# A graph network's edge stage: the order of a chunk's steps within and across slots, on one core

## The chip, the core and the metric

The kernel runs on one core of a Trainium2 chip. The metric is device time in microseconds, the median of several executions; smaller is better. The engines of the core are TensorE (PE in the profile, its weight loads PEld), VectorE (DVE), ScalarE (ACT), GpSimd (POOL) and SyncE (SP), each with its own instruction stream; they meet only at semaphores.

## What is computed

```python
# x (12500, 64), src, dst (400000,), dst sorted, edge_attr_16 (400000, 16)
x = layernorm(x + L0(x, src, dst))      # three graph convolutions with degree norms and ELU
x = layernorm(x + L1(x, src, dst, edge_attr_16))

# L1, of which the edge stage is the first three lines
ea = edge_attr @ W_edge.T + b_edge
msg = relu(x[src] + ea)                 # one message of 64 numbers for each of 400000 edges
agg = segment_sum(msg, dst, 12500)
h = (x + agg) @ W1.T + b1               # then batch statistics, relu, @ W2.T + b2
```

The destinations are skewed: node numbers are 12500 times the square of a uniform number, so the first nodes have many more edges than the last.

## The kernel before, in words

The first convolutions (L0) are done with dense matrices of edge counts, in the first 4650 us or so. While they run, the edges of the first 5 windows of 512 nodes are written out again, sorted by the block of 128 source nodes. The edge stage then takes the edges in two ways, interleaved.

A **unit** is 5 tiles of 128 edges, in the order given, for the later windows. GpSimd gathers the source rows from DRAM with 5 indirect DMAs (`gather_units`, L1086), into one of 6 row buffers. TensorE makes the edge term from the attributes (`unit_edges`, L2271), VectorE adds the gathered rows to it (`add_rows`, L1652) and builds 5 one-hots of the destination (`unit_hots`, L1660), ScalarE and VectorE split the rectified message in two halves of 16 bits (`unit_high`, L1934; `unit_low`, L1665), and TensorE adds them into the window's sums (`unit_sums`, L2285). There are 345 units. GpSimd may gather unit n once `add_rows` of unit n - 6 is done.

A **chunk** is 8 or 6 tiles of the sorted edges, 294 in all, 147 of each size. Its source rows come from a table in SBUF through a one-hot, not by a DMA. The steps, by helper:

- `prepare` (VectorE, L1634, L1637, L1638): the source's digit and the destination from the records.
- `spread_digits` (TensorE, L2304), in two halves of up to four tiles, both into one PSUM bank: each tile's digits spread over 128 partitions. `src_hot` turns them into one-hots: VectorE the first half (L1645), ScalarE the second in two steps (L1924, L1928). The second half of the spread waits for VectorE's `src_hot`, the next chunk's first half for ScalarE's.
- `chunk_flat` (ScalarE, L1908), `turn_attr` (TensorE, L2315), `chunk_attr` (ScalarE, L1917): the attributes, turned.
- `chunk_terms` (TensorE, L2324 and 12 or 16 times L2331): edge terms plus source rows. `chunk_high` (ScalarE, L1899) and `chunk_low` (VectorE, L1680): the two message halves.
- `chunk_hots` (VectorE, L1673, one of 512 columns for each tile): node one-hots. `chunk_sums` (TensorE, L2344, one for each tile): the sums.

The order of all this is written out by hand: each engine loops over slots n, one slot for each unit, and in 294 of them also stands work on chunks. `STEP_OF` spreads the chunks evenly, so about every seventh slot has none; `CHUNK_IN` gives the chunk of a slot. Most buffers of a chunk exist twice, and every helper begins with its waits. `ENDS_IN` says in which slot a window's sums are closed, multiplied by W1 and put into the batch statistics. SP loads attributes (L892) and records (L900), three ahead.

## Time and profile before

| | |
|---|---|
| median of 3 runs | 7608.19 us (7603.3 to 7616.36) |
| the profiled execution, first to last instruction (span) | 7586.7 us |
| mean granted TensorE clock over the span | 0.862 |
| PE / DVE / ACT / POOL busy | 73% / 56% / 30% / 50% of the span |
| DMA, mean | 109 GB/s |

The profiled execution's own time is given by its span alone; the median of the runs is 21.5 us above it. The page has the busy shares by slices of the span; a table of stretches gives busy times between two moments; groups put instructions of one line together; a timeline lists single instructions, and behind each what ended the idle time before it ("remote": something that the profile does not tell). TensorE's instructions overlap, and their ends are worked out by a model.

### The profile page before, as it was taken

Reading aid. Unit: us, or ns where it says so; the run is one execution under the profiler, and the core shown is the slowest. Engines: PE = TensorE matmul, PEld = TensorE weight load, DVE = VectorE, ACT = ScalarE, POOL = GpSimd, SP = SyncE. Lnnn points to the kernel's source line nnn. Section 1 sums busy time; section 2 is a strip of 40 time slices with the busy share of each in tenths; the row PEclk is TensorE's granted clock in tenths of the full one; section 3 lists DMA queues with packets and bytes.
Section 4 is the critical chain, followed back from the end, with each engine's and each line's share of the span. In section 5 each row is a group of like instructions: output and inputs, shape, how many; then the busy total and the mean of one; then the engine's idle time right before and its main releaser. Section 6 shows DMA issues by size and latency. Waiting matters only on the chain.

```text
span 7586.7 us, 112214 instructions
## 1 busy us (share of the span) xinstructions
PE 5556.9 (73%) x39907; PEld 3224.8 (43%) x39908; DVE 4274.3 (56%) x14548; ACT 2271.1 (30%) x4057; POOL 3774.9 (50%) x3824
## 2 busy tenths in 40 slices
PE   6599799997777777778777774666766666665666
PEld 5366566665433333333433332333433333333334
DVE  5488888899533333333444112666666665555556
ACT  2487688873100000000001111333333322222223
POOL 4323233354354544545554556565655666665663
PEclk9799899999888988888888886888888888878887
DMA  2333333331555655556556661111111111111111
GB/s 99 140 130 119 120 142 137 118 118 64 177 173 188 197 177 180 186 186 195 184 185 193 218 207 41 32 34 33 33 33 33 34 33 32 33 33 32 32 32 34
DMA packets 438341, 828.25 MB, mean 109 GB/s; under 512 B 161611, under 2 KB 266983, under 8 KB 430951
## 3 DMA queue, kind: packets, MB, share of 16 engines
q1 hardware_dynamic: 305430, 713.88, 27.9%
q0 software_dynamic: 117952, 81.54, 5.1%
q10 hardware_dynamic: 14400, 25.61, 1.2%
q8 instruction: 323, 5.29, 0.3%
q14 instruction: 236, 1.93, 0.1%
HBM read 621.34 MB, written 199.35 MB: 108 GB/s over the span
## 4 chain that ended last, share of the span: by engine, by line
PE 24%; another core or an unknown queue 14%; issue 13%; DVE 11%; PEld 2%; ACT 1%; PEldq 0%; DVEq 0%; ACTq 0%
PE banks L2182 10%; PE banks L2344 4%; DVE tmp L1673 4%; PE banks L2271 2%; PE banks L2304 2%; PEld banks L2182 2%; DVE onehot L1660 2%; DVE rows_f L1652 2%; PE banks L2324 2%; PE banks L2331 1%; PE banks L2164 1%; DVE rows_f L1680 1%; DVE rows_f L1665 1%; PE banks L2157 1%
## 5 line engine op out<-in xcount | busy, mean ns | idle before, releaser
L1086 POOL DMA_INDIRECT rows_f<-table,src_key x1725 | 1708.4, 990 | 1103.4 <-DVE rows_f L1652 604.3
L1051 POOL DMA_INDIRECT sorted_recs<-onehot,rows x1280 | 1235.5, 965 | 1260.6 <-DMA onehot<-edge_recs_dram 718.7
L2182 PE MATMUL banks<-wide,rows_f 128*128 128x512 fp8e4 (+1 forms) x4900 | 1268.1, 400 | 355.4 <-issue 352.3
L1867 ACT ACTIVATE wide<-banks 128x784 fp8e4<-128x784 f32 x1563 | 1205.6, 825 | 484.6 <-PE banks L2104 340.6
L1006 POOL DMA_INDIRECT onehot<-edge_runs_dram,rows_f x472 | 596.2, 1263 | 1149.1 <-DVE onehot L1196 935.9
L2104 PE MATMUL banks<-rows_f 128*128 128x196 f16 (+2 forms) x7525 | 1004.1, 258 | 223.6 <-ACT wide L1867 138.7
L2104 PEld LDWEIGHTS banks<-rows_f 128*128 128x128 f16 x7525 | 708.5, 152 | 612.1 <-ACT wide L1867 401.9
L2271 PE MATMUL banks<-w_edge_blk,rows 80*128 80x320 f32 x690 | 337.4, 578 | 762.9 <-DVE rows_f L1652 521.6
L1444 DVE SCALAR_TENSOR_TENSOR onehot<-banks,onehot 128x98 f16<-128x98 f32 (+2 forms) x1113 | 295.6, 266 | 989.9 <-PE banks L2164 504.1
L1342 DVE TENSOR_TENSOR rows_f<-hid 128x1024 f16<-128x1024 f16 (+1 forms) x1016 | 679.4, 669 | 300.8 <-PE banks L2104 169.5
L1645 DVE TENSOR_SCALAR rows_f<-banks,iota_p 128x512 f16<-128x512 f32 x294 | 220.7, 751 | 1067.0 <-remote 638.8
L2182 PEld LDWEIGHTS banks<-wide,rows_f 128*128 128x128 f16 x4900 | 454.9, 103 | 817.2 <-issue 510.3
L2069 PE MATMUL banks<-wide,onehot 128*128 128x392 fp8e4 x3125 | 791.5, 334 | 9.2 <-issue 8.9
L2182 PE MATMUL banks<-wide,hid 128*128 128x512 fp8e4 (+1 forms) x2450 | 650.1, 401 | 126.3 <-issue 125.2
L1347 DVE TENSOR_TENSOR rows_f<-rows_f,tmp 128x1568 f16<-128x1568 f16 (+1 forms) x874 | 714.4, 817 | 0.0
L2344 PE MATMUL banks<-tmp,rows_f 128*128 128x512 f16 x2058 | 676.6, 485 | 0.0
L1673 DVE TENSOR_SCALAR tmp<-iota_win,rows 128x512 f16<-128x512 f16 x2058 | 638.0, 379 | 0.0
L1899 ACT ACTIVATE rows_f<-banks 128x512 f16<-128x512 f32 (+1 forms) x294 | 160.0, 544 | 1146.8 <-remote 671.6
L2271 PEld LDWEIGHTS banks<-w_edge_blk,rows 80*128 80x128 f32 x690 | 126.0, 228 | 825.3 <-issue 824.7
L2157 PE MATMUL banks<-onehot 128*128 128x98 f16 (+2 forms) x1113 | 244.1, 219 | 160.2 <-DVE onehot L1444 101.1
L2344 PEld LDWEIGHTS banks<-tmp,rows_f 128*128 128x128 f16 x2058 | 233.5, 120 | 295.3 <-issue 198.3
L1660 DVE TENSOR_SCALAR onehot<-iota_win,dst_key 128x224 f16<-128x224 f16 x1725 | 353.6, 287 | 0.0
(345 smaller groups left out, 7312.1 us busy)
## 6 DMA issues: line engine op xcount, KB each, us to landing
wide<-counts SPq DMA_DIRECT2D x504, 896.0 KB
counts<-wide SPq DMA_DIRECT2D x50, 3136.0 KB
rows_f<-table,src_key POOLq DMA_INDIRECT x1725
sorted_recs<-onehot,rows POOLq DMA_INDIRECT x1280
sorted_recs<-rows SPq DMA_DIRECT2D x28, 640.0 KB
rows<-attr_dram SPq DMA_DIRECT2D x345, 40.0 KB
onehot<-edge_recs_dram SPq DMA_DIRECT2D x143, 90.0 KB
agg_a<-attr_dram ACTq DMA_DIRECT2D x50, 250.0 KB
```

Of the source, the lines that this page charges most:

```text
L1006: G.indirect_dma_start(out=stage[:, c % STAGES, j, :], out_offset=None, in_=edge_runs[:, :], in_offset=bass.IndirectOffsetOnAxis(ap=run_id ...
L1051: G.indirect_dma_start(out=sorted_recs[:, :], out_offset=bass.IndirectOffsetOnAxis(ap=keys_of(t, t + 1).bitcast(I32), axis=0), in_=taken[g ...
L1086: G.indirect_dma_start(out=g_rows[:, n % ROW_RING, k, :], out_offset=None, in_=table32[:, :], in_offset=bass.IndirectOffsetOnAxis(ap=src_k ...
L1342: V.tensor_tensor(lo_ring[:, s, :, 0:size], iota_lots[:, :, 0:size], lo_cols[:, n:lot.end].rearrange("p (o n) -> p o n", o=1).to_broadcast ...
L1347: V.tensor_tensor(key_ring[:, s, 0:size * cells].rearrange("p (n j e) -> p n j e", n=size, e=2), iota_key[:, 0:cells].rearrange("p (o j e) ...
L1673: last = V.tensor_scalar(c_hot[:, s, k, :], iota_win[:, :], c_dst[:, s, k:k + 1], None, ALU.is_equal)
L1867: A.activation(win_counts[o.half % 2][:, :, d0:d0 + o.quads * QUAD].rearrange("p b (q c) -> p b q c", c=QUAD), counted, ACT.Copy, scale=UN ...
L2069: M(out_ps.rearrange("p (b d) -> p b d", d=QUAD), ident16[:, :], win_counts[o.half % 2][:, :, d0:d0 + QUAD], start=False, stop=False)
L2104: last = M(octet_ps[n % 2][:, q, at:at + item.width * BLOCKS], lo, key, start=fresh[q], stop=True, skip_group_check=True)
L2182: last = M(acc_d[m % 2].rearrange("p (h d) -> p h d", h=2)[:, 0:h, :], layer_rows[n][:, block, :], pieces[:, PLACE[k], 0:h, c * HALF:(c + ...
L2271: M(g_ps, g_attr[:, n % ATTR_RING, :], w_edge_blk[0:UNIT * EDIM, 0:UNIT, :].rearrange("p k f -> p (k f)"), start=True, stop=True).then_inc ...
L2344: last = M(c_acc, c_two[:, s, k, :], c_hot[:, s, k, :], start=False, stop=False)
```

## The change

Three hand-written loops are reordered, on VectorE, ScalarE and TensorE; no instruction's size changes. In the slot of chunk j:

- TensorE spreads both halves of chunk j's digits (before: chunk j + 1's), with `unit_sums`, `unit_edges` and `turn_attr` between them, then makes the sums of chunk j - 2 (before: of j, after its terms), and last the terms of chunk j (before: first).
- VectorE begins with `add_rows` of the unit, then `src_hot(j)`, `chunk_low(j - 1)`, the unit's work, `chunk_hots(j - 1)` and `prepare(j + 1)`. Before, a slot began with `prepare(j + 1)`, `chunk_hots(j)` and `src_hot(j + 1)`, and `chunk_low(j)` followed `add_rows`.
- ScalarE makes `chunk_high(j - 1)`, and `src_hot(j)` in place of `src_hot(j + 1)`.
- There are two slots more, for the sums of the last two chunks.

```diff
--- before.py
+++ after.py
@@ -302,8 +302,11 @@
 
 CHUNKS_S = plan_chunks()
 
-STEP_OF = [n * GATHERS // len(CHUNKS_S) for n in range(len(CHUNKS_S))]
-CHUNK_IN = {step: j for j, step in enumerate(STEP_OF)}
+CHUNKS_N = len(CHUNKS_S)
+SUMS_LATER = 2
+STEP_OF = [n * GATHERS // CHUNKS_N for n in range(CHUNKS_N + SUMS_LATER)]
+SLOT_IN = {step: j for j, step in enumerate(STEP_OF)}
+STEPS = GATHERS + 1 + SUMS_LATER
 UNIT_NODES = 224
 
 
@@ -340,9 +343,9 @@
 UNIT_WINDOWS = [sorted({b // WIN, (b + UNIT_NODES - 1) // WIN}) for b in UNIT_BASE]
 BEGINS = {w: min(n for n in range(GATHERS) if w in UNIT_WINDOWS[n]) for w in range(SORTED, WINDOWS)}
 ENDS = {w: max(n for n in range(GATHERS) if w in UNIT_WINDOWS[n]) for w in range(SORTED, WINDOWS)}
-WINDOW_ENDS = sorted([(n + 1, 0, w) for w, n in ENDS.items()] + [(STEP_OF[j], 1, c.w) for j, c in enumerate(CHUNKS_S) if c.ends])
+WINDOW_ENDS = sorted([(n + 1, 0, w) for w, n in ENDS.items()] + [(STEP_OF[j + SUMS_LATER], 1, c.w) for j, c in enumerate(CHUNKS_S) if c.ends])
 END_OF = {w: q for q, (n, kind, w) in enumerate(WINDOW_ENDS)}
-ENDS_IN = {step: [q for q, e in enumerate(WINDOW_ENDS) if e[0] == step] for step in range(-1, GATHERS + 2)}
+ENDS_IN = {step: [q for q, e in enumerate(WINDOW_ENDS) if e[0] == step] for step in range(-2, STEPS)}
 
 LAST = 20
 ROW_RING, REC_RING, ATTR_RING, HOT_RING = 6, 4, 4, 4
@@ -907,8 +910,8 @@
                 for n in range(GATHERS):
                     if n + ATTR_RING - 1 < GATHERS:
                         load_attr(n + ATTR_RING - 1)
-                    if n in CHUNK_IN and CHUNK_IN[n] + REC_RING - 1 < len(CHUNKS_S):
-                        load_recs(CHUNK_IN[n] + REC_RING - 1)
+                    if n in SLOT_IN and SLOT_IN[n] + REC_RING - 1 < CHUNKS_N:
+                        load_recs(SLOT_IN[n] + REC_RING - 1)
 
             def unsorted_edges():
                 steps = sp.value_load(bounds[0:1, WINDOWS - 1, 1:2], min_val=1, max_val=WINDOWS * GRANULES)
@@ -1693,25 +1696,25 @@
                 gathered = dst_key[:, FIRST_UNIT * UNIT:].rearrange("p (g t) -> p g t", t=GRAN)
                 link(V.tensor_tensor(gathered, gathered, g_base.rearrange("p (g o) -> p g o", o=1).to_broadcast([P, len(BASES), GRAN]), ALU.subtract))
                 prepare(0)
-                src_hot(0)
                 dve.wait_ge(s_dtable, 16 * WINDOWS)
-                for n in range(GATHERS):
-                    j = CHUNK_IN.get(n)
-                    following = j is not None and j + 1 < len(CHUNKS_S)
-                    if following:
+                for n in range(STEPS):
+                    j = SLOT_IN.get(n)
+                    if n < GATHERS:
+                        add_rows(n)
+                    if j is not None and j < CHUNKS_N:
+                        src_hot(j)
+                    if j is not None and 1 <= j <= CHUNKS_N:
+                        chunk_low(j - 1)
+                    if n < GATHERS:
+                        unit_hots(n)
+                        unit_low(n)
+                    if j is not None and 1 <= j <= CHUNKS_N:
+                        chunk_hots(j - 1)
+                    if j is not None and j + 1 < CHUNKS_N:
                         prepare(j + 1)
-                    if j is not None:
-                        chunk_hots(j)
-                        if following:
-                            src_hot(j + 1)
-                    add_rows(n)
-                    if j is not None:
-                        chunk_low(j)
-                    unit_hots(n)
-                    unit_low(n)
-                    for q in ENDS_IN[n - 2] if n >= 1 else ():
-                        hidden_stats(q)
-                for n in range(GATHERS - 2, GATHERS + 2):
+                    for q in ENDS_IN[n - 2]:
+                        last = hidden_stats(q)
+                for n in range(STEPS - 2, STEPS):
                     for q in ENDS_IN[n]:
                         last = hidden_stats(q)
                 last.then_inc(s_tail, 1)
@@ -1948,19 +1951,17 @@
                 chunk_flat(0)
                 chunk_flat(1)
                 chunk_attr(0)
-                src_hot(0)
-                for n in range(GATHERS + 2):
-                    j = CHUNK_IN.get(n)
-                    following = j is not None and j + 1 < len(CHUNKS_S)
-                    if j is not None:
-                        chunk_high(j)
-                    if following:
-                        chunk_attr(j + 1)
+                for n in range(STEPS):
+                    j = SLOT_IN.get(n)
+                    if j is not None and 1 <= j <= CHUNKS_N:
+                        chunk_high(j - 1)
                     if n < GATHERS:
                         unit_high(n)
-                    if following:
-                        src_hot(j + 1)
-                    if j is not None and j + 2 < len(CHUNKS_S):
+                    if j is not None and j + 1 < CHUNKS_N:
+                        chunk_attr(j + 1)
+                    if j is not None and j < CHUNKS_N:
+                        src_hot(j)
+                    if j is not None and j + 2 < CHUNKS_N:
                         chunk_flat(j + 2)
                     for q in ENDS_IN[n - 1]:
                         window_hidden(q)
@@ -2361,28 +2362,27 @@
                 pe.wait_ge(s_dout, len(DENSE))
                 pe.wait_ge(s_x1two, X1TWO0 + 1)
                 unit_edges(0)
-                spread_digits(0, 0)
                 turn_attr(0)
-                spread_digits(0, 1)
-                for n in range(GATHERS + 2):
-                    j = CHUNK_IN.get(n)
-                    following = j is not None and j + 1 < len(CHUNKS_S)
-                    if j is not None:
-                        chunk_terms(j)
-                    if following:
-                        spread_digits(j + 1, 0)
-                        turn_attr(j + 1)
-                        turned[0] = j + 2
+                for n in range(STEPS):
+                    j = SLOT_IN.get(n)
+                    here = j is not None and j < CHUNKS_N
+                    if here:
+                        spread_digits(j, 0)
                     if 1 <= n <= GATHERS:
                         unit_sums(n - 1)
                     if n + 1 < GATHERS:
                         unit_edges(n + 1)
-                    if following:
-                        spread_digits(j + 1, 1)
+                    if here and j + 1 < CHUNKS_N:
+                        turn_attr(j + 1)
+                        turned[0] = j + 2
+                    if here:
+                        spread_digits(j, 1)
                     for q in ENDS_IN[n - 1]:
                         window_nodes(q)
-                    if j is not None:
-                        chunk_sums(j)
+                    if j is not None and j >= SUMS_LATER:
+                        chunk_sums(j - SUMS_LATER)
+                    if here:
+                        chunk_terms(j)
 
             pe.wait_ge(s_flag, 1)
             flagged = nc.tensor.value_load(flag[0:1, 0:1], min_val=0, max_val=1)
```

VectorE, a slot with a chunk of 8 tiles in the middle of the edge stage, before. `banks` is PSUM, `iota_win` and `iota_p` are counting numbers, `rows` holds digits and destinations. The row of L1645 is `src_hot`, the next one `add_rows`:

```order
7475 L1673 TENSOR_SCALAR tmp<-iota_win,rows 128x512 x8
7476 L1645 TENSOR_SCALAR rows_f<-banks,iota_p 128x512
7477 L1652 TENSOR_TENSOR rows_f<-banks,rows_f 128x320
7478 L1680 SCALAR_TENSOR_TENSOR rows_f<-banks,rows_f 128x8x64
7479 L1660 TENSOR_SCALAR onehot<-iota_win,dst_key 128x224 x5
7480 L1665 SCALAR_TENSOR_TENSOR rows_f<-rows_f 128x5x64
7481 L1634 TENSOR_SCALAR rows<-rows_f 128x8
7482 L1637 CAST rows<-rows 128x8
7483 L1638 TENSOR_SCALAR rows<-rows_f 128x8
7484 L1673 TENSOR_SCALAR tmp<-iota_win,rows 128x512 x8
```

and with the change, where lines have moved down by 3 (L1655 is `add_rows`, L1648 `src_hot`, L1683 `chunk_low`, L1663 the unit's one-hots, L1668 `unit_low`, L1676 the node one-hots, L1637 to L1641 `prepare`):

```order
7478 L1655 TENSOR_TENSOR rows_f<-banks,rows_f 128x320
7479 L1648 TENSOR_SCALAR rows_f<-banks,iota_p 128x512
7480 L1683 SCALAR_TENSOR_TENSOR rows_f<-banks,rows_f 128x8x64
7481 L1663 TENSOR_SCALAR onehot<-iota_win,dst_key 128x224 x5
7482 L1668 SCALAR_TENSOR_TENSOR rows_f<-rows_f 128x5x64
7483 L1676 TENSOR_SCALAR tmp<-iota_win,rows 128x512 x8
7484 L1637 TENSOR_SCALAR rows<-rows_f 128x8
7485 L1640 CAST rows<-rows 128x8
7486 L1641 TENSOR_SCALAR rows<-rows_f 128x8
7487 L1655 TENSOR_TENSOR rows_f<-banks,rows_f 128x320
```

`src_hot` stood between the node one-hots and `add_rows`; now it stands behind `add_rows`, and all the slot's other work lies between it and the next `add_rows`.

TensorE, one slot before, from `chunk_terms` (L2324, L2331) over the first half of the spread (L2304), `turn_attr` (L2315), `unit_sums` (L2285), `unit_edges` (L2271) and the second half to `chunk_sums` (L2344):

```order
8649 L2324 MATMUL banks<-w_edge_blk,rows 128x512
8650 L2331 MATMUL banks<-hid,rows_f 128x64 x16
8651 L2304 MATMUL banks<-rows 128x128 x4
8652 L2315 MATMUL banks<-ident,rows 128x128
8653 L2285 MATMUL banks<-onehot,rows_f 128x224 x5
8654 L2271 MATMUL banks<-w_edge_blk,rows 128x320
8655 L2304 MATMUL banks<-rows 128x128 x4
8656 L2344 MATMUL banks<-tmp,rows_f 128x512 x8
```

and with the change, where lines have moved down by 1:

```order
8669 L2305 MATMUL banks<-rows 128x128 x4
8670 L2286 MATMUL banks<-onehot,rows_f 128x224 x5
8671 L2272 MATMUL banks<-w_edge_blk,rows 128x320
8672 L2316 MATMUL banks<-ident,rows 128x128
8673 L2305 MATMUL banks<-rows 128x128 x4
8674 L2345 MATMUL banks<-tmp,rows_f 128x512 x8
8675 L2325 MATMUL banks<-w_edge_blk,rows 128x512
8676 L2332 MATMUL banks<-hid,rows_f 128x64 x16
```

The rows are the same but for `turn_attr`, which has moved behind `unit_edges`; what has moved is which chunk they belong to: both rows of L2305 are now of the chunk of the terms that follow them, and the eight sums are of the chunk two earlier.

## Rows read from the trace of the kernel before

**Rows 1.** The page, GpSimd's busy tenths in 40 slices of 190 us.
```profile
POOL 4323233354354544545554556565655666665663
```

**Rows 2.** Table of stretches, the edge stage. Columns: stretch, length, busy us and count of PE, PEld, DVE, ACT, POOL, granted clock, DMA share, GB/s.
```profile
4680.00:7520.00 2840.00, 1863.72 (x12809) 1092.71 (x12809) 1710.94 (x5972) 811.98 (x1866) 1704.80 (x1723) 0.82 0.14 32
```

**Rows 3.** Groups of instructions, 4680 to 7520 us: count, busy us, mean ns, idle before, releasers.
```profile
L1086 POOL DMA_INDIRECT rows_f<-table,src_key x1723 | 1704.8, 989 | 1103.0 <-DVE rows_f L1652 604.3 <-issue 498.6
```

**Rows 4.** Waits, 4680 to 7520 us: engine and line, releaser, us in total, times, longest.
```profile
DVE rows_f L1645 <- remote: 638.8, 169, 35.2
POOL rows_f L1086 <- DVE rows_f L1652: 604.3, 211, 6.9
...
DVE rows_f L1645 <- PE banks L2304: 404.9, 112, 10.1
```

**Rows 5.** Timeline of GpSimd, one slot: start, duration, line, idle before and releaser.
```profile
5308.91 0.95 POOL L1086 DMA_INDIRECT rows_f<-table,src_key  x1 [2.35 <-DVE rows_f L1652]
...
5314.22 0.95 POOL L1086 DMA_INDIRECT rows_f<-table,src_key  x1 [0.30 <-issue]
```

**Rows 6.** Timeline of VectorE, the same slot.
```profile
5308.15 0.48 DVE L1652 TENSOR_TENSOR rows_f<-banks,rows_f 128x320 f32<-128x320 f32 x1
5308.55 0.68 DVE L1680 SCALAR_TENSOR_TENSOR rows_f<-banks,rows_f 128x512 f16<-128x512 f32 x1
5309.15 1.02 DVE L1660 TENSOR_SCALAR onehot<-iota_win,dst_key 128x224 f16<-128x224 f16 x5
5310.09 0.49 DVE L1665 SCALAR_TENSOR_TENSOR rows_f<-rows_f 128x320 f16<-128x320 f32 x1
5310.49 0.17 DVE L1634 TENSOR_SCALAR rows<-rows_f 128x8 int32<-128x8 int32 x1
...
5310.85 2.45 DVE L1673 TENSOR_SCALAR tmp<-iota_win,rows 128x512 f16<-128x512 f16 x8
5316.06 0.75 DVE L1645 TENSOR_SCALAR rows_f<-banks,iota_p 128x512 f16<-128x512 f32 x1 [2.77 <-remote]
5316.73 0.48 DVE L1652 TENSOR_TENSOR rows_f<-banks,rows_f 128x320 f32<-128x320 f32 x1
```

**Rows 7.** Timeline of TensorE, the same slot.
```profile
5309.40 0.39 PE L2304 MATMUL banks<-rows 128*128 128x128 f16 x4
5309.62 1.89 PE L2344 MATMUL banks<-tmp,rows_f 128*128 128x512 f16 x8
...
5312.67 0.39 PE L2304 MATMUL banks<-rows 128*128 128x128 f16 x4
...
5313.17 0.64 PE L2285 MATMUL banks<-onehot,rows_f 128*128 128x224 f16 x5
```

**Rows 8.** Timeline of ScalarE, the same slot.
```profile
5309.82 0.69 ACT L1924 ACTIVATE rows_f<-banks,iota_p 128x512 f16<-128x512 f32 x1 [0.68 <-PE banks L2304]
```

**Rows 9.** Timeline, a slot whose gathers have ended.
```profile
5289.03 0.94 POOL L1086 DMA_INDIRECT rows_f<-table,src_key  x1 [0.30 <-issue]
...
5290.64 0.39 PE L2304 MATMUL banks<-rows 128*128 128x128 f16 x4
...
5291.07 0.75 DVE L1645 TENSOR_SCALAR rows_f<-banks,iota_p 128x512 f16<-128x512 f32 x1 [2.96 <-PE banks L2304]
```

**Rows 10.** Timeline, three units' gathers in a row.
```profile
5326.11 0.95 POOL L1086 DMA_INDIRECT rows_f<-table,src_key  x1 [2.38 <-DVE rows_f L1652]
...
5337.54 0.75 DVE L1645 TENSOR_SCALAR rows_f<-banks,iota_p 128x512 f16<-128x512 f32 x1 [5.39 <-remote]
...
5344.32 0.94 POOL L1086 DMA_INDIRECT rows_f<-table,src_key  x1 [0.30 <-issue]
...
5347.57 0.69 ACT L1924 ACTIVATE rows_f<-banks,iota_p 128x512 f16<-128x512 f32 x1 [8.37 <-remote]
```

**Rows 11.** Timeline, two units' gathers in a row.
```profile
5384.25 0.95 POOL L1086 DMA_INDIRECT rows_f<-table,src_key  x1 [0.94 <-issue]
...
5398.82 0.75 DVE L1645 TENSOR_SCALAR rows_f<-banks,iota_p 128x512 f16<-128x512 f32 x1 [5.57 <-remote]
```

## The prediction

> **What bounds the kernel now.** I read the page's slices first, then the table of stretches, the groups of instructions and the waits of the edge stage, and last the timeline of single slots. The edge stage is the stretch from 4680 to 7520 us, 2840 of the 7586.7 us [rows 2], and the change touches nothing else. The page's slices show GpSimd half busy in all of it [rows 1]. No engine is full: TensorE is busy for 1863.7 us, VectorE for 1710.9, GpSimd for 1704.8, and the DMA share is 0.14 [rows 2]. So the stage is bound by waits, and the question is which wait ends last.
>
> GpSimd only issues row gathers, 1723 of 989 ns, and between units it waits 604 us for `add_rows` (L1652) to free a buffer [rows 3, 4]. VectorE waits 639 + 405 us in front of `src_hot` (L1645) [rows 4]. `src_hot` stands just ahead of `add_rows` on VectorE, so these are one loop: `add_rows`, five gathers, something that holds `src_hot`, `src_hot`, `add_rows`.
>
> What holds it? `src_hot` needs `spread_digits` (L2304) of TensorE. In the slot shown TensorE's row ends at 5312.67 + 0.39 = 5313.06 [rows 7], yet `src_hot` starts at 5316.06, after VectorE stood idle for 2.77 us [rows 6]. The five gathers started at 5308.91 [rows 5], 7.15 us before it. In a slot where GpSimd had finished (last gather 5289.03 + 0.94 = 5289.97), the same rows read 5290.64 + 0.39 = 5291.03 and 5291.07: no delay at all [rows 9]. And where three units' gathers stand in a row, 15 from 5326.11 to 5344.32, ScalarE's wait on a spread ends at 5347.57, 21.46 us after the first [rows 10]. 7.15 / 5 = 1.43 and 21.46 / 15 = 1.43. **My reading:** each gather occupies something for 1.43 us, and while such work is outstanding TensorE's completion signals reach the others late, at one of its boundaries, often only at the last one. A signal early in a burst still passes: ScalarE starts L1924 at 5309.82 [rows 8], 0.03 us after TensorE's row ends (5309.40 + 0.39) [rows 7], though the first gather started at 5308.91. What the thing is, the trace does not say. The Trainium skill, page Perfetto Trace Analysis, summary of the profiler window per engine type, says that TensorE's end in a trace is estimated and that semaphore propagation lies outside it; rows 9 agree with an end that is nearly exact when GpSimd is quiet, and no row gives the page's own length for the propagation.
>
> The loop's period today, with 8 tiles: 7.15 from first gather to `src_hot`, then 5316.73 - 5316.06 = 0.67 for it, and 5308.91 - 5308.15 = 0.76 from the start of `add_rows` to the first gather: 8.58 us, and the two `add_rows` shown are 8.58 apart [rows 5, 6]. The loop is in phase with itself: the one signal that VectorE waits for comes at the end of the burst, and nothing but 1.4 us stands between it and the next burst.
>
> **The change, part by part.** (1) No instruction is added or taken away; loads, gathers and matmuls keep their sizes and counts. (2) Chunk sums, node one-hots and message halves come a slot or two later. That removes the waits of TensorE inside a slot. TensorE was not what ended the slot (its rows end at 5313.06 and a bit, [rows 7]), so alone this is worth 0; if its cover went, it would cost at most one slot's eight sums, 1.89 us [rows 7]. (3) Two slots more at the end, for the last two chunks' sums: they hold no gathers, and I charge 7 us once (bounds 0 and 2 x 8.58). SP's record loads keep their rule, one per chunk, and wait for `prepare`, which now ends the slot instead of opening it: three chunks ahead, some 25 us, against a burst of gathers of 7: cost 0, and if that cover went, a late load would cost a slot once in a while.
>
> (4) What matters is VectorE's order. Now `add_rows(n)` comes first and `src_hot(j)` right behind it, then `chunk_low`, the unit's one-hots, `unit_low`, eight node one-hots and `prepare`. So what stands between the release of `src_hot` and the next `add_rows` grows from `src_hot` alone to: `src_hot` 0.67, `chunk_low` 0.60 (5308.55 to 5309.15), unit one-hots 0.94 (to 5310.09), `unit_low` 0.40 (to 5310.49), `prepare` 0.36 (to 5310.85), node one-hots 2.45 [rows 6]: **5.42 us**. This work ran under the burst before. It still can, but only if `src_hot` is not held when the burst starts.
>
> (5) Whether it is held depends on two TensorE signals in series in each slot, since the digits are spread in their own slot: first half of the spread, `src_hot`, second half, ScalarE's far half (two steps, the first 0.69, so 1.4 in all, [rows 8]), `chunk_terms` (1.2, from the sums' end at 5311.51 to 5312.67, [rows 7]), first half of the next chunk's spread. If GpSimd is quiet the whole round takes 0.67 + 0.39 + 1.89 (the sums, which cover the 1.4) + 1.2 + 0.39 = 4.5 us, shorter than VectorE's 5.42, so the next `src_hot` finds its signal there: one good slot of 5.42 + 0.4 (`add_rows`, 5308.15 to 5308.55) = 5.8 us. But 5.8 is less than the 7.15 that its gathers occupy. In that slot the round's signals are emitted inside the burst, the last of them 4.5 us or more after its start, and the next `add_rows` joins five more gathers to it: ten in a row. The next `src_hot` is then held until a late boundary of ten. The trace has both ends for this. One at 5337.54 - 5326.11 = 11.43 (8 x 1.43) [rows 10]; the other where two units stand together: first gather 5384.25, `src_hot` 5398.82, 14.57 [rows 11]. Then 5.42, and 0.76 to the next first gather. So **two slots take 17.6 us (8.8 each) or 20.75 (10.4 each)** with 8 tiles; with 6 tiles, half the chunks, node one-hots fall by 0.61 and `chunk_low` by about 0.15: 8.4 or 10.0 each.
>
> **The sum.** 294 slots hold a chunk, 51 only a unit, which adds its gathers' 7.15. Low end: 147 x 8.8 + 147 x 8.4 + 51 x 7.15 = 2893 us. High end: 147 x 10.4 + 147 x 10.0 + 365 = 3364. Today's `add_rows` are 345 x 8.18 = 2822 apart in all (345 into 2840 less the ends, [rows 2]). I take the pair held to the last boundary in one case of four, since the shorter wait is the one after which TensorE's work is done: 2893 + 0.25 x 471 = 3011, so +189, and +7 for the tail: **+196**. The profiled execution's span is 7586.7 us; the median of the runs shown is 7608.19, 21.5 above it for what lies around the span and the spread of 13 us over three runs. 7608 + 196 = 7804, which I round to **7800**.
>
> **Rivals.** *Faster, the signals get through.* If TensorE, which now runs ahead, emits each slot's signals early in a burst, `src_hot` is never held and the 5.42 us hide. The stage then goes at 5 x 1.43 = 7.15 per unit: 345 x 7.15 = 2467, -355, so about 7260; with every second slot so, 7430. It decides from the point where the round of (5) ends within some 2.5 us of the first gather. For it: L1924 above got through at 0.9 us [rows 8]. Against: the round is 4.5 us long and a slot 5.8. The Trainium skill, page Perfetto Trace Analysis, Optimization Strategy, advises to find what ends the gaps of the most-contended engine and start it sooner; followed here without the delay of signals, GpSimd's waits would vanish and leave its issue alone, the case just priced, and no row shows that regime held.
>
> *No change.* Both orders have one `src_hot` and two spreads per slot. If bad and good slots average out (5.8 + 11.4 = 17.2 against 2 x 8.58 = 17.16), the stage stays within 15 us of today. The chunkless slots speak against it: they already make ten or fifteen gathers in a row [rows 10, 11], and would then meet pairs.
>
> *Slower by more.* If the ten gathers join a further five regularly, the wait is 21.46 for three slots plus 6.2, 9.2 each, or the 20.75 pairs prevail: 7900 to 8150. TensorE's clock is no rival: granted 0.82 in the stage [rows 2], and in the slot shown nothing of its own ends after 5313.81 (5313.17 + 0.64), 2.2 us before `src_hot` [rows 7].
>
> *The change does not do what it says.* The orders above show that it does: `chunk_sums` stands two chunks behind. 0.
>
> **How the numbers follow.** This kernel's measurement can tell about 0.2% (15 us) from no change. Forecast, slower by pairing: 0.58 (7650 to 8000). Slower by more: 0.08. Within 0.2%: 0.08. Faster: 0.26, half of it below 7450. The range leaves out the lower half of the faster case (0.13) and the worst of the slower (0.05): 7450 to 8030; the forecast's own range is 7650 to 8000.
>
> **What would show it.** Right: intervals of `add_rows` that alternate, near 6 and near 12 us; gathers in runs of ten; the idle time of VectorE in front of `src_hot` still near 1000 us although it stands elsewhere; GpSimd's wait for `add_rows` up from 604 to some 800 us; gathers still 989 ns. Wrong: even intervals near 7.2 and `src_hot` never idle (faster), or waits in front of `add_rows` itself on TensorE's edge terms (another loop). If VectorE's or TensorE's own durations change, the sum is wrong in its terms.

## The result, and the profile after

The changed kernel takes 7774.64 us (median of 4 runs, 7762.45 to 7782.07), the kernel before beside it 7607.90: **1.0216 times, 95% interval 1.0197 to 1.0235**. That is +167 us against +192 forecast (7800), inside the range. In two later jobs the ratio was 1.0179 (1.0140 to 1.0219) and 1.0123 (1.0092 to 1.0154). Its profiled execution has a span of 7768.4 us and took 7770.4. One of the runs below, the sixth of experiment 6, took 7217.68 us at a granted clock of 0.675 where the others had 0.887 to 0.893, and is left out of its median.

In the changed kernel the lines of ScalarE, GpSimd and VectorE stand 3 further on (`add_rows` L1655, `src_hot` L1648, gathers L1089, the far half of `src_hot` L1927 and L1931) and TensorE's one (spread L2305, terms L2332, sums L2345, edge terms L2272). The table of stretches, from its first `add_rows` to its end:

```profile
4745.00:7700.00 2955.00, 1839.80 (x12809) 1109.24 (x12808) 1672.12 (x5969) 786.14 (x1863) 1706.63 (x1723) 0.79 0.16 31
```

Against [rows 2] hardly anything works longer: TensorE's weight loads are busy 17 us more and its matmuls 24 us less, VectorE 39 us less, GpSimd the same. The stage is longer by waits. Groups of instructions, 4740 to 7700 us:

```profile
L1089 POOL DMA_INDIRECT rows_f<-table,src_key x1725 | 1710.0, 991 | 1212.7 <-DVE rows_f L1655 743.0 <-issue 469.6
L1648 DVE TENSOR_SCALAR rows_f<-banks,iota_p 128x512 f16<-128x512 f32 x294 | 220.3, 749 | 980.4 <-remote 617.0 <-PE banks L2305 348.0 <-issue 13.5
L1655 DVE TENSOR_TENSOR rows_f<-banks,rows_f 128x320 f32<-128x320 f32 x345 | 167.1, 484 | 275.0 <-issue 228.6 <-remote 37.0 <-PE banks L2272 6.0
```

GpSimd's gathers still take 991 ns, and its wait for `add_rows` grew from 604 to 743 us [rows 3, 4]. `src_hot` still waits some 1000 us (980 against 639 + 405 in [rows 4]). New is the third row: `add_rows` itself now waits 275 us, most of it put down to "issue", for which the profile shows no reason (the one is found below). In the kernel before, the same group reads:

```profile
L1652 DVE TENSOR_TENSOR rows_f<-banks,rows_f 128x320 f32<-128x320 f32 x345 | 166.0, 481 | 6.5 <-issue 6.1
```

**Where in the program.** From the first of the 345 `add_rows` to the last is 2821.3 us before and 2937.2 after: the edge stage costs **+115.9**. From the last `add_rows` to the end of the span it is 79.0 and 81.9: +2.9. The other 63 us lie ahead of the stage, where the first `add_rows` starts (timelines of both kernels):

```profile
4686.34 0.48 DVE L1652 TENSOR_TENSOR rows_f<-banks,rows_f 128x320 f32<-128x320 f32 x1
```
```profile
4749.27 0.49 DVE L1655 TENSOR_TENSOR rows_f<-banks,rows_f 128x320 f32<-128x320 f32 x1 [4.44 <-issue]
```

The code up to there is the same in both, but for the first chunk's spreads and its `src_hot`. Experiments 1 to 8 below, on two chips, leave that part alone too, and their first `add_rows` fell at 4645, 4716, 4728, 4742, 4719, 4735, 4722 and 4664 us. So the start of the stage differs by up to 97 us between single profiles of such kernels, and the 63 us cannot be laid to the change; the stage is best compared by itself. What makes the 63 us stays open: within this job the runs of either kernel lie only 13 and 20 us apart, so it is not scatter from one execution to the next. A stage is also known from one execution alone, and the kernel before has a profile in the first job only.

**How the gathers run.** A burst is a row of gathers with no wait longer than 0.75 us between them. Counted from the starts and ends of all 1725 gathers, with the mean time per gather from a burst's first gather to the next burst's:

| kernel | first to last `add_rows`, us | bursts of 5 (us per gather) | of 10 | of 15 | longer |
|---|---|---|---|---|---|
| before | 2821.3 | 215 (1.641) | 32 (1.584) | 19 (1.671) | 1 |
| changed | 2937.2 | 119 (1.731) | 59 (1.673) | 20 (1.772) | 10 |

Joined bursts are 1.7 times as many, and yet a joined burst is not dearer per gather than a single one. By their means each kind has become dearer by 0.09 to 0.10 us per gather. The means hide where it sits. The next table sorts the same bursts by the VectorE instruction that stood idle for more than 0.3 us between a burst's last gather and the next burst; each entry is a count and the mean time from first gather to next first gather (bursts of 15 and more are left out):

| | held at `src_hot` | held at `add_rows` | held at neither |
|---|---|---|---|
| before, bursts of 5 | 215, 8.20 us | none | none |
| changed, bursts of 5 | 14, 12.85 us | 15, 7.90 us | 90, 8.13 us |
| before, bursts of 10 | 32, 15.84 us | none | none |
| changed, bursts of 10 | 21, 19.54 us | 29, 15.03 us | 9, 15.64 us |

A burst at whose end `src_hot` stands is dear now, by 4.6 us (5) and 3.7 us (10), since VectorE's longer piece of work only starts then; all others in the table cost as much as before or less. The 35 dear ones take 143 us more than at the old means, which is about the size of the loss. The other two profiles of the changed kernel (experiments 5 and 12) repeat it: 8 and 14 bursts of five at 13.0 and 13.2 us, 35 and 32 of ten at 19.3 and 19.7.

One pair of units in the timeline of the changed kernel shows how a pair held at `add_rows` runs:

```profile
5418.17 0.94 POOL L1089 DMA_INDIRECT rows_f<-table,src_key  x1 [7.31 <-DVE rows_f L1655]
...
5421.04 0.49 DVE L1655 TENSOR_TENSOR rows_f<-banks,rows_f 128x320 f32<-128x320 f32 x1 [1.80 <-issue]
...
5421.68 0.78 PE L2272 MATMUL banks<-w_edge_blk,rows 80*128 80x320 f32 x2 [1.22 <-DVE rows_f L1655]
...
5422.42 0.75 DVE L1648 TENSOR_SCALAR rows_f<-banks,iota_p 128x512 f16<-128x512 f32 x1 [0.89 <-remote]
...
5423.23 0.40 PE L2305 MATMUL banks<-rows 128*128 128x128 f16 x4 [0.56 <-issue]
...
5429.43 0.94 POOL L1089 DMA_INDIRECT rows_f<-table,src_key  x1 [0.30 <-issue]
5432.35 0.49 DVE L1655 TENSOR_TENSOR rows_f<-banks,rows_f 128x320 f32<-128x320 f32 x1 [4.46 <-issue]
5432.50 0.69 ACT L1927 ACTIVATE rows_f<-banks,iota_p 128x512 f16<-128x512 f32 x1
5433.11 0.94 POOL L1089 DMA_INDIRECT rows_f<-table,src_key  x1 [2.73 <-DVE rows_f L1655]
5433.22 0.72 ACT L1931 ACTIVATE rows_f<-rows_f,ones_col 128x512 f16<-128x512 f16 x1
...
5434.09 1.01 PE L2332 MATMUL banks<-hid,rows_f 128*128 128x64 f16 x16 [6.19 <-ACT rows_f L1931]
...
5434.91 0.61 PE L2305 MATMUL banks<-rows 128*128 128x128 f16 x4
...
5435.92 0.75 DVE L1648 TENSOR_SCALAR rows_f<-banks,iota_p 128x512 f16<-128x512 f32 x1 [3.08 <-PE banks L2305]
...
5441.04 0.48 DVE L1655 TENSOR_TENSOR rows_f<-banks,rows_f 128x320 f32<-128x320 f32 x1
...
5441.80 0.94 POOL L1089 DMA_INDIRECT rows_f<-table,src_key  x1 [2.71 <-DVE rows_f L1655]
```

Ten gathers start at 5418.17. `add_rows` and `src_hot` come inside the burst, the second half of the spread ends at 5423.63 and the unit's edge terms (L2272) at 5422.46. Their signals arrive late, as if at the burst's last boundary: `add_rows` starts at 5432.35 and ScalarE's L1927 at 5432.50, 14.18 and 14.33 us after the first gather, 10 x 1.43 = 14.3. `add_rows` frees the next burst (5433.11), 14.94 us after the first gather of this one. But ScalarE's two steps, the terms and the next spread only now follow one another, and `src_hot` starts 3.57 us behind `add_rows`. The next burst of five is under way by then; `src_hot` and what follows it take 5.1 us up to the next `add_rows`, and the burst's period is 5441.80 - 5433.11 = 8.69. That VectorE's own signal is not held shows in the same lines: TensorE's L2272 starts at 5421.68, 0.15 us after `add_rows` ends (5421.04 + 0.49), in the middle of the burst.

**The signals themselves.** The traces also record when most semaphores were updated, which shows the late signals directly. In the lines above the semaphore of the edge terms was updated at 5432.27 and that of the spread at 5432.37, 9.8 and 8.7 us after their rows end. Over the edge stage of the kernel before, 575 of the 588 updates of the spread can be matched to their matmuls. Of these 249 came within 0.1 us of the matmul's end and 282 more than 1 us later, the longest 20.9 us. Of the 322 that came later than 0.1 us and whose matmul ended inside a burst (1.43 us counted for each gather), 239 came within 0.15 us of a multiple of 1.43 us from the first gather, where chance would give 68; of the 42 whose matmul ended outside a burst, 38 came within 0.1 us. VectorE's updates are not held: of `unit_low` 311 are recorded, 306 of them inside bursts, and all came within 0.1 us. A trace does not tell whether the signal or the matmul itself is late, since TensorE's ends are modelled; for the waits it comes to the same.

### The profile page after: what moved, and what is told of

Read it like the earlier page. It is cut to its first block, busy times and chain, and to the rows that moved or that the text cites. A ratio compares the mean times of both kernels' runs of the same rounds, so it can differ in the third digit from the quotient of the medians.

```text
span 7768.4 us, 112213 instructions
## 1 busy us (share of the span) xinstructions
PE 5563.3 (72%) x39907; PEld 3254.7 (42%) x39908; DVE 4239.1 (55%) x14548; ACT 2246.6 (29%) x4057; POOL 3772.0 (49%) x3824
## 4 chain that ended last, share of the span: by engine, by line
PE 23%; another core or an unknown queue 18%; issue 12%; DVE 9%; ACT 2%; PEld 2%; PEldq 0%; DVEq 0%; POOL 0%; DMA 0%; ACTq 0%
PE banks L2183 12%; PE banks L2345 3%; DVE tmp L1676 3%; PEld banks L2183 2%; PE banks L2332 2%; DVE rows_f L1648 1%; DVE onehot L1663 1%; PE banks L2305 1%; PE banks L2165 1%; PE banks L2325 1%; PE banks L2158 1%; ACT rows_f L1927 1%; ACT rows_f L1931 1%; DVE rows_f L1683 1%
## 5 line engine op out<-in xcount | busy, mean ns | idle before, releaser
L1089 POOL DMA_INDIRECT rows_f<-table,src_key x1725 | 1710.0, 991 | 1212.7 <-DVE rows_f L1655 743.0
L2070 PE MATMUL banks<-wide,onehot 128*128 128x392 fp8e4 x3125 | 793.1, 334 | 13.2 <-issue 12.9
L1648 DVE TENSOR_SCALAR rows_f<-banks,iota_p 128x512 f16<-128x512 f32 x294 | 220.3, 749 | 980.4 <-remote 617.0
L2345 PE MATMUL banks<-tmp,rows_f 128*128 128x512 f16 x2058 | 632.6, 459 | 0.0
L1676 DVE TENSOR_SCALAR tmp<-iota_win,rows 128x512 f16<-128x512 f16 x2058 | 595.0, 358 | 0.0
L2305 PE MATMUL banks<-rows 128*128 128x128 f16 x2058 | 251.2, 247 | 468.2 <-DVE rows_f L1648 366.3
L2332 PE MATMUL banks<-hid,rows_f 128*128 128x64 f16 x4116 | 188.5, 202 | 444.3 <-ACT rows_f L1931 351.8
L2332 PEld LDWEIGHTS banks<-hid,rows_f 128*128 128x128 f16 x4116 | 168.8, 104 | 640.1 <-issue 634.0
L2272 PE MATMUL banks<-w_edge_blk,rows 80*128 80x320 f32 x690 | 316.9, 544 | 129.6 <-DVE rows_f L1655 60.1
```

The costliest lines, as they stand in the source:

```text
L1089: G.indirect_dma_start(out=g_rows[:, n % ROW_RING, k, :], out_offset=None, in_=table32[:, :], in_offset=bass.IndirectOffsetOnAxis(ap=src_k ...
L1676: last = V.tensor_scalar(c_hot[:, s, k, :], iota_win[:, :], c_dst[:, s, k:k + 1], None, ALU.is_equal)
L2070: M(out_ps.rearrange("p (b d) -> p b d", d=QUAD), ident16[:, :], win_counts[o.half % 2][:, :, d0:d0 + QUAD], start=False, stop=False)
L2332: last = M(c_ps[s][:, k * D:(k + 1) * D], hot, x1_two[:, c.blocks[k // c.tiles], part * D:(part + 1) * D], start=False, stop=True, skip_gr ...
L2345: last = M(c_acc, c_two[:, s, k, :], c_hot[:, s, k, :], start=False, stop=False)
```

## The experiments

Each "stage" below is from one profiled execution of its kernel, mostly in another job than the 2821.3 us of the kernel before, whose median was 7646.68 us in the job of experiments 1 to 4 and 7622.53 in that of 5 to 8. Differences of 30 us between stages are not resolved by that. Theory A is the prediction's: TensorE's signals are late while gathers are outstanding, and VectorE's longer piece of work between `src_hot`'s release and the next `add_rows` turns that into longer periods. The rivals are that the loss comes from the later sums, one-hots and halves; that the engines' waits on each other in the new order cost it, whatever GpSimd does; that gathers fit into GpSimd's idle time; and that a part of the loss is outside the edge stage. Each expectation gives them its letters. "Stage" is always first to last `add_rows`.

**1. `src_hot` ahead of `add_rows` again,** in the changed kernel; all else of the change stays.

```diff
-                    if n < GATHERS:
-                        add_rows(n)
                     if j is not None and j < CHUNKS_N:
                         src_hot(j)
+                    if n < GATHERS:
+                        add_rows(n)
```

> The changed kernel with one pair of steps exchanged on VectorE: src_hot(j) stands ahead of add_rows(n) again; TensorE and ScalarE keep the new order. Theory A (late signals while gathers are outstanding, and VectorE's 5.4 us of work between src_hot and the next add_rows): the burst of gathers then starts 1.4 us after src_hot is released as before, pairs of bursts vanish, the edge stage's add_rows span falls from 2937 back to 2820 to 2860 us, and the time to 7610 to 7700. Rival B (the loss lies in TensorE's new order, two spreads and the terms in series within one slot): stays at 7740 to 7790.

Measured: 7652.02 us, 1.0006 times the kernel before (0.9985 to 1.0027), stage 2848.9 in an execution of 7577.64, the fastest of eleven. The swap of two calls takes the loss away. Its `add_rows` waits 2.9 us, not 275:

```profile
L1655 DVE TENSOR_TENSOR rows_f<-banks,rows_f 128x320 f32<-128x320 f32 x345 | 165.9, 481 | 2.9 <-DMA rows_f<-table,src_key 2.9
L1089 POOL DMA_INDIRECT rows_f<-table,src_key x1723 | 1723.9, 1001 | 1100.5 <-DVE rows_f L1655 611.6 <-issue 489.0
```

Bursts: 203 of five, 34 of ten. The later sums, one-hots and halves, and the two slots more, are thus worth nothing either way while this order is kept.

**2. `src_hot` behind `add_rows`,** in the kernel before.

```diff
                         chunk_hots(j)
-                        if following:
-                            src_hot(j + 1)
                     add_rows(n)
+                    if following:
+                        src_hot(j + 1)
```

> The kernel before with one pair of steps exchanged on VectorE: src_hot(j + 1) stands behind add_rows(n) instead of ahead of it, nothing else moves. Theory A: nearly the whole loss comes with this alone: add_rows span 2900 to 2970 us, time 7700 to 7780, gathers in runs of ten. Rival B (TensorE's order is what costs): within 20 us of 7608.

Measured: 7675.88 us, 1.0054 (1.0023 to 1.0086), stage 2850.9, 159 bursts of five and 67 of ten. Slower, but by far less than expected, 0.5% where Theory A had nearly the whole loss; the stage is 30 us above the 2821.3, not 79 to 149, and next to the 2848.9 of experiment 1 in the same job it is no longer at all. `add_rows` waits 182.6 us here: the new wait comes with the order, its price needs something else of the change as well.

**3 and 4. Six gathers a unit, and three,** in the kernel before. The sixth repeats the unit's last tile into an unused place; with three, tiles 3 and 4 of a unit are not gathered. `add_rows` waits for the number issued.

```diff
-                    for k in range(UNIT):
+                    for k in range(3):
```

> The kernel before with a sixth gather per unit (a copy of the fifth, into a spare place that nobody reads). Theory A (each gather holds TensorE's signals 1.43 us and the loop runs through it): 345 x 1.43 = 493 us more, so 8040 to 8120; the interval of add_rows in full slots goes from 8.58 to 10.0. Rival C (the gathers are off the path: GpSimd waits 604 us for buffers and has room for 345 x 1.25 = 431 us more): 7600 to 7660.

> The kernel before with three of a unit's five gathers; the messages of tiles 3 and 4 of each unit are left wrong, all other work stays. Theory A: the loop falls to 3 x 1.43 + 1.43 = 5.7 us, under VectorE's own 5.9 with 8 tiles and 5.2 with 6, so the stage falls to 1950 to 2100 and the time to 6750 to 6900. Rival C: 7590 to 7620.

Measured, one execution each: 8145.48 us and stage 3336.1 with six, 25 us above A's band, but +499 us against the kernel before in the same job, where A had +493; 6827.91 and 2004.8 with three, within its bands. The 345 gathers more are busy for 328 us, and GpSimd had been idle for 1103 us [rows 3], enough for all of them. It costs (3336.1 - 2821.3) / 345 = 1.49 us a unit. The idle time did not take them up. The groups of the kernel with six:

```profile
L1086 POOL DMA_INDIRECT rows_f<-table,src_key x1723 | 1691.2, 982 | 1192.6 <-DVE rows_f L1655 674.9 <-issue 517.7
L1089 POOL DMA_INDIRECT tmp<-table,src_key x345 | 328.1, 951 | 105.2 <-issue 105.2
L1648 DVE TENSOR_SCALAR rows_f<-banks,iota_p 128x512 f16<-128x512 f32 x294 | 220.7, 751 | 1519.1 <-remote 894.4 <-PE banks L2307 603.4 <-issue 21.4
```

`src_hot`'s wait grows from 1067 to 1519 us. With three gathers it is 304.0. So what `src_hot` waits for is the burst, at some 1.43 us per gather, and not TensorE's work, which is the same in all three.

**5. The changed kernel again,** in another job.

> The changed kernel itself, once more, for a second trace and a comparison on the same chip. A (the loss sits in the edge stage, by the order of add_rows and src_hot): the first add_rows may start anywhere between 4640 and 4760 us, since that varied among kernels that are identical up to there, but first to last add_rows is again 2920 to 2955 us against 2821 of the kernel before; 1.012 to 1.022 times the kernel before. D (the 63 us by which the changed kernel entered the edge stage later belong to the change): first add_rows again at 4740 us or later, and 1.020 or more.

Measured: 7761.70 us against 7622.53, 1.0179 (1.0140 to 1.0219). The first `add_rows` fell at 4718.85, so D falls; the stage took 2981.7 us, longer than A's band. Its `add_rows` waits 213.9 us, GpSimd for it 800.6; its bursts of 5, 10, 15 and more number 87, 63, 30 and 9.

**6. The changed kernel with three gathers.** The edit is that of experiment 4.

> The changed kernel with three gathers a unit instead of five (tiles 3 and 4 of a unit are not gathered, so their messages are wrong), against 6827.9 us and an edge stage of 2004.8 us of the kernel before with three. A (the order of add_rows and src_hot costs only through signals that are held while gathers are outstanding): three gathers occupy 4.3 us, less than the 5.4 us of VectorE work behind src_hot, so the new order costs little: edge stage 1990 to 2060 us, 6790 to 6900 us. C (the new order costs by its own waits among the engines): the same 116 us as with five gathers: edge stage 2110 us or more, 6930 to 6960 us.

Measured: 6845.6 us (five runs), stage 2058.3: 53.5 more than with three gathers in the order of before, which was one execution on another chip. A's band for the stage ends at 2060, and C's numbers (2110 or more, 6930 or more) are not met; a third to a half of the loss stays where a burst is two fifths shorter, and `add_rows` waits only 18.6 us. Signals are held here too: of 512 matched updates of the spread 104 came more than 1 us late.

**7. Each chunk's sums one chunk later on TensorE,** in the kernel before, nothing else moved.

```diff
...
+SUMS_IN = {step: j for j, step in enumerate(STEP_OF[1:])}
...
-                    if j is not None:
-                        chunk_sums(j)
+                    if n in SUMS_IN:
+                        chunk_sums(SUMS_IN[n])
```

> The kernel before, with each chunk's sums one chunk later on TensorE and nothing else changed. A (only a longer piece of work behind src_hot loses time): 0.997 to 1.003 times the kernel before, edge stage 2800 to 2840 us. C (sums that come later are what the changed kernel loses by, since the node one-hots and halves are then freed a slot later): 1.01 or more.

Measured: 7640.55 us, 1.0031 (1.0009 to 1.0053), stage 2833.4: small, but clear of nothing; C's 1.01 is excluded. But the wait has moved. The node one-hots need the buffer of sums that now come later, and take over half of what `src_hot` waited (groups of this kernel):

```profile
L1674 DVE TENSOR_SCALAR tmp<-iota_win,rows 128x512 f16<-128x512 f16 x2058 | 627.1, 374 | 554.6 <-remote 241.1 <-PE banks L2345 185.4 <-issue 127.8
...
L1646 DVE TENSOR_SCALAR rows_f<-banks,iota_p 128x512 f16<-128x512 f32 x294 | 220.4, 750 | 527.0 <-remote 466.9 <-PE banks L2305 49.9 <-issue 9.9
```

554.6 + 527.0 = 1081.6, against 1067.0 of `src_hot` alone in the kernel before. It matters little which TensorE signal VectorE stands at; it stands there until the burst is over.

**8. Both edits, 2 and 7.**

> The kernel before, with src_hot behind add_rows (which alone gave 1.0054) and with each chunk's sums one chunk later on TensorE. A1 (the two together are what the change is; with its sums out of the way TensorE's signals fall earlier in a burst and pairs of bursts form more often): edge stage 2915 to 2955 us, 1.012 to 1.020. A2 (the rest of the loss is in ScalarE's order or in the late node one-hots and prepare): as the one with src_hot behind alone, 2840 to 2865 us, 1.003 to 1.008.

Measured: 7737.21 us, 1.0159 (1.0127 to 1.0191), stage 2946.2, 63 bursts of five and **103 of ten**, these at 1.717 us per gather. Alone the two edits give 0.54% and 0.31%; together 1.59%. That is the size of the change, and A1's numbers (the change itself has its sums two chunks later, not one), but not by quite the change's waits: here the node one-hots wait 461.0 us and `add_rows` 65.4. A pair in its timeline:

```profile
5094.86 0.95 POOL L1087 DMA_INDIRECT rows_f<-table,src_key  x1 [2.90 <-DVE rows_f L1653]
...
5099.14 0.48 DVE L1653 TENSOR_TENSOR rows_f<-banks,rows_f 128x320 f32<-128x320 f32 x1
...
5106.31 0.95 POOL L1087 DMA_INDIRECT rows_f<-table,src_key  x1 [0.30 <-issue]
...
5109.15 2.19 DVE L1674 TENSOR_SCALAR tmp<-iota_win,rows 128x512 f16<-128x512 f16 x8 [4.87 <-remote]
5111.26 0.48 DVE L1653 TENSOR_TENSOR rows_f<-banks,rows_f 128x320 f32<-128x320 f32 x1
5112.01 0.95 POOL L1087 DMA_INDIRECT rows_f<-table,src_key  x1 [4.76 <-DVE rows_f L1653]
```

The one-hots are released 14.29 us after the first gather (10 x 1.43), then 2.19 of work, and the pair takes 17.15: the shape that the forecast described, with other work in `src_hot`'s place.

**9 to 11. A spread that comes earlier; one gather a unit in both orders.** Experiment 9 was meant to be a version that beats both.

```diff
-                        spread_digits(j + 1, 0)
                         turn_attr(j + 1)
...
+                    if j is not None and j + 2 < len(CHUNKS_S):
+                        spread_digits(j + 2, 0)
                     if j is not None:
                         chunk_sums(j)
```

> The kernel before, with the first half of a chunk's digits spread right behind the second half of the chunk ahead of it, before eight sums and the terms that stood between, and with prepare one slot earlier for it. In the slot shown the signal for src_hot would then be given some 2.0 us after the first gather instead of 4.2. F (a signal that early in a burst often gets through, so src_hot is released inside the burst and a burst follows at once): edge stage 2600 to 2760 us, 0.965 to 0.992 times the kernel before. H (it is held to the burst's end as before; the work moved is hidden either way): 2800 to 2840 us, 0.997 to 1.003. P (bursts join in pairs, as in the changed kernel): 2880 us or more, 1.008 or more.

> The kernel before with one gather a unit (tiles 1 to 4 of a unit are not gathered, so their messages are wrong). With three the edge stage took 2004.8 us, 5.8 a slot, against 4.9 us of VectorE work a slot; with one both theories expect 1850 to 1990 us. It is the measure for the next one.

> The changed kernel with one gather a unit. A (the new order costs only where signals are held while gathers are outstanding; one gather occupies 1.43 us): edge stage within 20 us of the kernel before with one gather, and the step from five gathers (116 to 160 us) by three (54 us) to one goes on towards nothing. C (a part of the loss, the 54 us that three gathers left, are waits of the engines on each other in the new order, whatever GpSimd does): 40 us or more slower than the kernel before with one gather.

Measured: experiment 9 took 5959.65 us, 1.0043 (1.0030 to 1.0057) times the kernel before, and **the kernel before took 5934.42 us here** (9 runs, 5929 to 5944), the same program that took 7622.53 in the job of experiments 5 to 8. One gather a unit: stage 1664.2 in the order of before, 1670.8 in the changed one, 5423.54 and 5429.80 us. In this job the signals were not held: in experiment 9 all 584 matched updates of the spread came within 0.02 us of its end, and with one gather a unit all 588 in either order. In the timeline of experiment 9 GpSimd never stops, and ScalarE starts 0.04 us after the spread's end (4712.21 + 0.39 = 4712.60):

```profile
4710.33 0.94 POOL L1086 DMA_INDIRECT rows_f<-table,src_key  x1 [0.30 <-issue]
4711.58 0.94 POOL L1086 DMA_INDIRECT rows_f<-table,src_key  x1 [0.30 <-issue]
...
4712.21 0.39 PE L2305 MATMUL banks<-rows 128*128 128x128 f16 x4
...
4712.64 0.69 ACT L1925 ACTIVATE rows_f<-banks,iota_p 128x512 f16<-128x512 f32 x1 [0.66 <-PE banks L2305]
4712.82 0.94 POOL L1086 DMA_INDIRECT rows_f<-table,src_key  x1 [0.30 <-issue]
```

and its groups, 3670 to 5890 us:

```profile
L1645 DVE TENSOR_SCALAR rows_f<-banks,iota_p 128x512 f16<-128x512 f32 x294 | 216.7, 737 | 2.0 <-PE banks L2305 2.0
L1652 DVE TENSOR_TENSOR rows_f<-banks,rows_f 128x320 f32<-128x320 f32 x345 | 167.9, 487 | 387.1 <-DMA rows_f<-table,src_key 386.5
L1086 POOL DMA_INDIRECT rows_f<-table,src_key x1724 | 1680.9, 975 | 525.5 <-issue 525.5
```

Stage 2200.3 us. `src_hot` waits 2.0 us; `add_rows` waits for its own gathers, and GpSimd's issue is the bound (1680.9 + 525.5 = 2206.4). This is the regime of the *faster* rival, reached without a change to the kernel, and faster than that was priced: 2200.3 / 344 = 6.4 us a unit, where 5 x 1.43 = 7.15 was charged. Whether the early spread helps where signals are held was not measured: F, H and P stay open. That the two orders differ by 6.6 us with one gather says that the order costs nearly nothing by itself when no signal is held; since the signals and the number of gathers changed together, it does not say which of the two took the 54 us of experiment 6 away.

**12. The changed kernel a third time.**

> The changed kernel a third time, beside the kernel before. In the job of the three runs before this one the kernel before took 5934 us instead of 7623: its gathers ran on without a gap, and in the trace of the early spread ScalarE's wait on a spread ended 0.04 us after TensorE's row, in the middle of gathers, so no signal was held. A (the change costs only by held signals): if the kernel before is again near 5934 us, the changed kernel is within 0.3% of it, edge stage within 10 us of 2200, gathers in one unbroken run; if it is near 7620 us, 1.014 to 1.022 as twice before. C (the new order costs by itself when five gathers run): 1.01 or more in either case.

Measured: before 7750.23 us, changed 7851.63, 1.0123 (1.0092 to 1.0154), stage 3008.2, the first `add_rows` at 4794.52. The signals were held again, and the loss is a little under A's band. What the change does where they are not held, with five gathers, was not measured.

## Why the prediction was right, and where not

- **What bounds the kernel.** Held up. Per gather 1.43 us (estimated), 1.49 from the sixth gather; the wait before `src_hot` follows the number of gathers (304, 1067 and 1519 us for three, five and six), and in the job where signals came at once the same program was 22% faster, though not by the edge stage alone (last section). The updates recorded in the traces show the held signals directly; what holds them stays open.
- **(1), no instruction's cost.** Right: gathers 991 ns against 989. VectorE's busy time even fell, by 43 us in the node one-hots (638.0 to 595.0), which the sum did not have; hidden.
- **(2), later sums and halves: 0.** Right in experiment 1; the sums alone, one chunk later, cost 0.3% (experiment 7). In the full change they are not neutral: with `src_hot` behind they triple the loss (0.54 to 1.59%). The prediction treated the parts as separate terms and charged VectorE's order with everything; the runs show an interaction.
- **(3), the tail: +7.** Measured +2.9. SP's loads cost nothing that shows.
- **(4), the longer piece between `src_hot` and `add_rows`.** The cause, shown by experiment 1 and by the bursts held at `src_hot`, which are the only ones to have become dear: 12.85 us for five gathers, where the prediction's terms give 7.15 + 5.42 + 0.76 = 13.3 with 8 tiles and 12.6 with 6.
- **(5), pairs.** Right in kind, wrong in form. Expected were 147 pairs, with 8 tiles at 17.6 us and a quarter of them at 20.75; found were 59 runs of ten at a mean of 16.7. The step that failed is "the next `src_hot` is then held until a late boundary of ten", then 5.42. That happened in 21 of the 59 pairs (19.54 us, near the 20.0 to 20.75 given for the last boundary) and, not forecast, behind 14 single bursts (12.85 us). In 29 pairs it is `add_rows` itself that is held, by the unit's edge terms, and goes at once when the burst ends (15.0 us, cheaper than the 15.84 of a pair before). What was missed is that signal, and the chain behind it, ScalarE's far half, terms and spread, 3.57 us in the rows above, which runs into the next burst. Fewer and cheaper pairs, and some single bursts made dear: 8.54 us a unit over all (2937.2 / 344), where 8.73 (3011 / 345) were forecast and 8.20 measured before.
- **The sum.** It was +189 for the stage and +7 behind it; the profiles have +116 and +3. That the medians, +167, lie near the forecast is luck in part: 63 us of the difference between the profiles stand ahead of the stage, where the prediction had nothing and the change moves only the first chunk's spreads and `src_hot`.
- **The test lines.** Alternation near 6 and 12 us: only in part; of the 344 intervals 152 lie between 5 and 8 us (77 before) and 73 between 8 and 10 (158 before), but between 11 and 14 there are 38, no more than the 42 before; above 14 there are 29 (8 before). Runs of ten: more, 59 against 32, not the rule. `src_hot` idle near 1000 us: yes, 980. GpSimd's wait at 800: 743 here, 801 and 844 in the other two profiles. A wait in front of `add_rows` on edge terms was named as a sign of error, and it is there, 275 us; in the pair shown the update of the edge terms' semaphore at 5432.27, 0.08 us ahead of `add_rows`, says that it is these.
- **The rivals.** *Faster*: no such thing in the three jobs where the changed kernel ran with held signals; its regime exists, but came without the new order. *No change*: excluded by three intervals. *Slower by more*: no.

## What to carry to other kernels

When a wait ends at a multiple of another engine's burst and not when its producer ends, count what stands on the waiting engine between that wait and the instruction that starts the next burst: here moving one call across another, with the sums already later, took away a loss of 1.2 to 2.2%, and by itself it cost 0.5%, while 39 us less of VectorE's busy time were worth nothing. Before adding up the parts of a reorder, run them alone and together: 0.5% and 0.3% made 1.6%. And compare the stage by itself, from its first to its last instruction; its start differed by up to 97 us between profiles with the same code ahead of it. Look at the slowest bursts one by one, too: a mean of 8.65 us against 8.20 was 14 bursts of 12.85 among 105 that had not become slower.

## What was not expected of the hardware

The same program took 7608 to 7750 us in four jobs and 5934 us in a fifth, which ran on the same chip as experiments 5 to 8, 29 minutes later. In the fifth TensorE's signals arrived within 0.04 us while GpSimd's gathers ran. The part ahead of the edge stage was shorter as well: first `add_rows` at 3676 us, not 4645 to 4795. There the stretch from 1950 to 3600 us is the clearest pair, experiment 5 above and experiment 9 below (the last three columns are the granted clock, the DMA share and GB/s):

```profile
1950.00:3600.00 1650.00, 1230.82 (x6854) 590.15 (x6852) 610.42 (x3842) 45.36 (x90) 802.88 (x833) 0.86 0.58 182
```
```profile
1950.00:3600.00 1650.00, 1614.99 (x9872) 835.71 (x9869) 908.63 (x5055) 136.16 (x212) 1234.14 (x1278) 1.00 0.85 276
```

Every engine does more in the same time there, and the granted clock is 1.00 (all of it at 2.4 GHz) instead of 0.86. In the edge stage the clock was 0.90 in experiment 9 against 0.82 in the kernel before [rows 2], and TensorE was busy for 184 us less (1679.5 against 1863.7), well under the 621 us by which that stage was shorter; so the clock alone is not the difference. The cause of the held signals is not visible in any profile, and what changed between the jobs is open.
